# The last layer of a four-layer model: expert tiles written back to their tokens at once and spread over more slots, value products moved between two pairs of scores

## The reference, cut to what matters

```python
# attention, 16 heads of 8 features, causal
qkv = (xn @ W_qkv + b_qkv).reshape(b, s, 16, 24)        # q, k, v of each head
attn = softmax(where(k_pos > q_pos, -inf, q @ k.T / sqrt(8)))
a = (attn @ v).reshape(b, s, 128) @ W_out + b_out
# experts: 8 of them, each token uses the two with the largest probability
probs = softmax(xn @ router_w.T);  top_p, top_i = top_k(probs, 2)
cw = one_hot(top_i) * top_p / (top_p.sum() + 1e-8)
for e in range(8):
    out += cw[:, e] * (gelu(xn @ w1[e].T + b1[e]) @ w2[e].T + b2[e])   # 128 -> 512 -> 128
x = x + a + out
```

## Time and profile before

| | |
|---|---|
| runs | 2456.61, 2458.77, 2468.96 us; median 2458.77 |
| profiled execution | span 2438.6 us from its first to its last instruction; what lies around it is not in the trace |
| mean granted TensorE clock | 0.899 of full speed |
| PE busy | 1961.1 us (80%) |
| DVE busy | 1854.7 us (76%) |
| ACT busy | 1448.4 us (59%) |
| POOL busy | 1318.1 us (54%) |
| layer 3's slots 3 to 15 | 1738.3 to 2358.8 us |
| its slots 16 to 18 | 2358.8 to 2438.6 us |

### The profile page before, as it was taken

The page is one execution under the profiler, slowest core; times in us unless marked ns, Lnnn a source line. Parts: engine busy times, 40 slices in busy tenths (PEclk is TensorE's granted clock), DMA queues, the critical chain, the costliest instruction groups (busy, mean ns, idle before and its releaser), DMA issues. The chain is left out here.

```text
span 2438.6 us, 32864 instructions
## 1 busy us (share of the span) xinstructions
PE 1961.1 (80%) x10212; PEld 1020.8 (42%) x10212; DVE 1854.7 (76%) x2464; ACT 1448.4 (59%) x2630; POOL 1318.1 (54%) x962
## 2 busy tenths in 40 slices
PE   6797797979797977879857999656688889898876
PEld 5233343433343333335625777532244544454322
DVE  6499999999999999878787888757465555645752
ACT  2676777767777775563546666312566566655655
POOL 5599999989898989322324554327411111111653
PEclk9898999989898988989888999855899998999978
DMA  2354444545444545300200000022222322322211
GB/s 72 99 160 138 155 144 146 150 154 164 140 142 146 157 140 158 123 27 1 85 0 1 0 0 0 5 76 83 82 75 83 108 77 66 92 68 76 57 44 30
DMA packets 150288, 214.84 MB, mean 88 GB/s; under 512 B 30970, under 2 KB 62612, under 8 KB 149524
## 3 DMA queue, kind: packets, MB, share of 16 engines
q1 hardware_dynamic: 146052, 204.72, 27.8%
q0 software_dynamic: 4096, 8.40, 1.3%
HBM read 193.91 MB, written 23.86 MB: 89 GB/s over the span
## 5 line engine op out<-in xcount | busy, mean ns | idle before, releaser
L717 PE MATMUL ps<-m_hC,ident 128*128 128x512 f32 x1024 | 518.0, 651 | 127.7 <-DVE m_hC L1005 127.7
L914 POOL TENSOR_TENSOR m_dBx<-m_du,m_rowB 128x1024 f32<-128x1024 f32 x256 | 604.0, 2391 | 5.9 <-DMA m_rowB<-bc_rows 5.6
L2909 DVE TENSOR_REDUCE a_mx<-ps 128x2 f32<-128x1024 f32 (+2 forms) x320 | 351.6, 1117 | 183.6 <-PE ps L2571 142.5
L2770 ACT ACTIVATE a_pT<-ps 128x512 f32<-128x512 f32 (+2 forms) x640 | 319.8, 553 | 287.2 <-PE ps L2593 279.5
L840 ACT ACTIVATE ps<-m_delta,m_A 128x512 f32<-128x512 f32 x512 | 339.7, 685 | 119.5 <-DVE m_h L996 118.6
L717 PEld LDWEIGHTS ps<-m_hC,ident 128*128 128x128 f32 x1024 | 207.1, 209 | 423.9 <-issue 237.3
L3056 POOL TENSOR_SCALAR_AFFINE_SELECT a_pT<-a_pT 128x512 f32<-128x512 f32 x128 | 81.5, 636 | 472.0 <-ACT a_pT L2770 471.5
L996 DVE TENSOR_TENSOR_SCAN m_h<-ps,m_carry,m_dBx 128x512 f32<-128x512 f32 x256 | 311.2, 1265 | 9.0 <-ACT ps L840 9.0
L996 DVE TENSOR_TENSOR_SCAN m_h<-ps,m_dBx 128x512 f32<-128x512 f32 x256 | 295.9, 1206 | 18.8 <-ACT ps L840 18.2
L924 POOL TENSOR_TENSOR m_hC<-m_h,m_rowC 128x1024 f32<-128x1024 f32 x80 | 194.6, 2433 | 70.4 <-DVE m_h L996 70.0
L1005 DVE TENSOR_TENSOR m_hC<-m_h,ps 128x1024 f32<-128x1024 f32 x176 | 214.9, 1221 | 21.2 <-ACT ps L850 7.2
(11 more groups left out here) (404 smaller groups left out, 3568.8 us busy)
## 6 DMA issues: line engine op xcount, KB each, us to landing
m_rowB<-bc_rows SPq DMA_DIRECT2D x256, 256.0 KB, 4.4
m_rowC<-bc_rows SPq DMA_DIRECT2D x256, 256.0 KB, 4.0
a_w<-in_L3f_w1T SPq DMA_DIRECT2D x39, 256.0 KB, 2.7
a_w<-in_L3f_w2T SPq DMA_DIRECT2D x39, 256.0 KB, 3.4
qk_parts<-a_part SPq DMA_DIRECT2D x24, 256.0 KB
expert_rows<-in_zero_rows SPq DMA_DIRECT2D x39, 128.0 KB, 2.6
a_xs<-expert_rows SPq DMA_DIRECT2D x39, 128.0 KB, 2.3
expert_out<-a_y SPq DMA_DIRECT2D x39, 128.0 KB, 3.3
```

The source lines that it names most:

```text
L717: mm = pe.matmul(ps[:, bankY + c, :], k.ident[:], hC[:, n % NBUF, c, :], start=False, stop=n % NS == NS - 1)
L914: pool.tensor_tensor(dBx[:, n % NBUF], du[:, i % 2, :, chunk(i, x)], rowB[:, n % 4, :].unsqueeze(1).to_broadcast([P, HALF, CH]), ALU.mult) ...
L2770: act.activation(dst, src, ACT.Exp).then_inc(t_read, 1)
L2909: dve.tensor_reduce(mx[:, c % 2, :, es[0]:es[0] + len(es), t, x // CH], src, AX_X, ALU.max)\
```

## The change

1. `scatter` now carries 129 words for each row: the token's 128 features and, in word 128, its place in the result (the token's number for its first expert, the number plus 4096 for its second). `expert_rows` is 129 words wide, its padding rows are filled from a larger input with numbers past 8191, and POOL adds 4096 to the numbers between the 32nd and the 33rd scatter, after waiting for the first 32 to land.
2. DVE casts a tile's 2 x 128 numbers to integers (`back`) when XT has arrived. Instead of SP's `store_tile` POOL issues two indirect DMAs for each tile (`put`), which write its rows to their tokens' places. `ys` has six buffers instead of two and lies in the space of `xn`. The puts of a slot's tiles come in groups 4 to 6 of the next slot; those of the last slot's tiles in groups 8 to 10 of slot 16.
3. The 64 gathers go. SP loads each sequence's rows with two plain DMAs of 512 KB (`bring`) after all puts have landed, two sequences ahead of `combine` at most. All four combines are in slot 17 (groups 6, 8, 10, 11).
4. The tiles go over slots 3 to 16: three in each, two in slots 5, 9 and 15.
5. In each group `sums` of the group before it comes between pair A and pair B, not after B; XT and DOWN come after B, DOWN last in the group. Group 4 takes four score pieces (groups 5 and 6 one each), and three of them lie between the UPs of its tiles.

```diff
-SHARE = (2, 2, 1, 1, 2, 2, 2, 2, 2, 2, 1, 1)
+SHARE = (2, 2, 1, 1, 4, 1, 1, 2, 2, 2, 1, 1)
-FIRST_SLOT, LAST_SLOT = 3, 12
+FIRST_SLOT, LAST_SLOT = 3, 16
-GATHER = {LAST_SLOT + 1 + n: n for n in range(B)}
+TILES_IN = (3, 3, 2, 3, 3, 3, 2, 3, 3, 3, 3, 3, 2, 3)
+COMBINE = {6: 0, 8: 1, 10: 2, 11: 3}
@@ SP
-                def store_tile(kt):
...
+                def bring(n):
+                    if n >= 2:
+                        sp.wait_ge(combined, (n - 1) * 16)
+                    for r in range(2):
+                        first = r * TOK + n * S
+                        sp.dma_start(got[:, n % 2, r], R["out_rows"][first:first + S, :].rearrange("(j p) d -> p j d", p=P))\
+                          .then_inc(s_g[n % 2], 16)
...
+                for u in range(NY):
+                    sp.wait_ge(s_y[u], 32 * len(range(u, NTILE, NY)))
+                for n in range(B):
+                    bring(n)
@@ PE, in a group (scoreT(b, g, 0) and the first score stand before this)
+                        if back and g > 0:
+                            sums(b, g - 1)
+                        if g == 0 and 0 <= b - 1:
+                            sums(b - 1, GROUPS - 1)
+                        if back and len(TU[g]) > 2:
+                            scoreT(b, g, 2)
                         for j, kt in enumerate(tiles_of(s)):
                             if g == j:
                                 turn_rows(kt)
-                            if g == 7 + j:
-                                down(kt)
-                        if back and len(TU[g]) > 2:
-                            scoreT(b, g, 2)
-                        for i in units[1:]:
+                        for i in units[1:] if g != BURST else ():
                             score(f, i)
...
-                        if back and g > 0:
-                            sums(b, g - 1)
...
+                        for j, kt in enumerate(tiles_of(s)):
+                            if g == 7 + j:
+                                down(kt)
                         if g == BURST:
+                            between = iter(units[1:])
                             for kt in tiles_of(s):
                                 for x in range(2):
                                     up(kt, x)
+                                    if x == 1:
+                                        for i in itertools.islice(between, 1):
+                                            score(f, i)
@@ DVE
+                    dve.tensor_copy(R["back"][:, 2 * kt:2 * kt + 2], xs[:, kt % 4, :, D])
...
+                        if s == SLOTS - 1 and g in COMBINE:
+                            combine(COMBINE[g])
-                    if s - 1 in GATHER:
-                        combine(GATHER[s - 1])
@@ POOL
+                def put(kt):
+                    pool.wait_ge(s_read, s_at["DOWN", kt] + 1)
+                    for a in range(2):
+                        pool.indirect_dma_start(R["out_rows"], bass.IndirectOffsetOnAxis(
+                            ap=R["back"][:, 2 * kt + a:2 * kt + a + 1], axis=0), ys[:, kt % NY, a, :], None)\
+                            .then_inc(s_y[kt % NY], 16)
...
+                        if n == NT:
+                            pool.wait_ge(R["scattered"], 16 * NT)
+                            pool.tensor_scalar(R["xn"][:, :, D], R["xn"][:, :, D], float(TOK), None, ALU.add)\
+                                .then_inc(numbered, 1)
+                            pool.wait_ge(numbered, 2)
...
+                            for j, kt in enumerate(tiles_of(s - 1)):
+                                if g == 4 + j and s < LAST_SLOT + 1:
+                                    put(kt)
+                            for j, kt in enumerate(tiles_of(s)):
+                                if g == 8 + j and s == LAST_SLOT:
+                                    put(kt)
```

105 lines of the change are left out of this document (51 added, 54 removed).

## The result

The changed kernel takes 2452.39 us (median of 20 runs, 2443.11 to 2460.59), the kernel before in the same session 2459.78. The ratio is 0.9974, with a 95% interval of 0.9962 to 0.9987. By the ratio that is 6.4 us less (the two medians lie 7.4 apart), a third of the 19 that were forecast. The profiled execution took 2455.94 us with a span of 2454.2.

A forecast was written before the change was run, and what follows sets the result against it. Slots 0 to 2 were taken as bound by POOL, groups with `down` by PE. Terms -14.3 - 10.8 - 13 + 2.4 + 6 + 7 + 3 = -19.7, taken as -19, gave 2440 us (-0.8%), range 2420 to 2462.

The forecast's parts named there:

- the sentence on the puts: Groups 4 to 6 of slots with tiles: POOL's 78 puts, 7.5 us a slot, fall where no mask is due: 0.
- The order: Slots 3 to 15: groups 5 and 6 fall from 7.22 to 4.8 us; taken as -1.0 a slot, -13 us.
- rival C: Slots with tiles: the order gives its whole -2.4 us a slot, time 2422 us; chance 0.15.
- Tiles and the excess of slots 14 and 15: Slots 3 to 15: three tiles leave for slot 16, -14.3 us; slots 14 and 15 lose their excess, -10.8 us.
- Slot 2: Slots 0 to 2: POOL is the bound, and the wait ahead of the 33rd scatter adds 2.4 us (0 to 4).
- The end: Slot 16 onward: +6 us for slot 16, +7 for late combines, +3 for slow passes.
- Slot 16: Slot 16 with three tiles and late puts between masks takes 40.8 us instead of 34.9: +6 (3 to 9).
- the +7: Slot 17: four combines in a chain, waiting for loads, end 7.2 us late and delay the last `norm`: +7 us.
- the +3: Behind the last `norm`: ten more projection pass pairs at half clock, 0.31 us each: +3 us (0 to 5).
- Rival A: Slots with tiles: the order gives nothing, as mask waits and a slower burst eat the gain; 2453 us; chance 0.20.
- D: Scatters in slots 0 to 2: the wider row costs POOL time, up to 0.95 us a scatter, 2501 us; chance 0.08.
- B: The end: a longer chain, loads of 9 us a pair (+7), slot with puts +3, slow passes +2; 2452 us; chance 0.12.

The follow-up runs named there:

- paced kernel: Changed kernel with GpSimd waiting, ahead of each tile's two puts, until ScalarE has done that group's exponentials: 2426.68 us, ratio 0.9833; on the quick chip 0.9944.
- c_seg: Changed kernel with the first 32 scatters counted in two semaphores, so the wait ahead of the 33rd is split: 2452.15 us, ratio 0.9978.
- d_tail: Changed kernel with the four combines moved to slot 17 behind groups 4, 5 and 6 and to slot 18: 2446.60 us, ratio 0.9942.
- h_best: Changed kernel with split scatter wait, combines moved to groups without masks, and the old place of `sums` in slots without tiles: 2434.32 us, ratio 0.9882.
- three tiles a slot with the three repairs: Changed kernel with split scatter wait, old `sums` place without tiles, three tiles in slots 3 to 15, combines in slots 16 and 17: 2428.46 us, 0.9854.

## Why the prediction was wrong, step by step

**The step that failed is the sentence on the puts**: "POOL's puts, 78 at the scatter's 0.95 + 0.30, lie in groups 4 to 6, where no mask is due and group 4 alone lasts 10 us; 7.5 a slot: 0." I asked whether GpSimd had time and who waits for it. It has, and nobody does. But six of them in a row hold up two other engines, which cost 27 us instead of 0. No row of the first profile showed this. Its execution lay 20.2 us under the median, which I took for time around the span, where the profile of after has 1.7 us around its own. That was a sign that most executions contain something that this one lacked, among it VectorE's stops in slots 0 and 2.

**The order**: -13 was too small. In slots 3 to 12 the kernel before with the order takes 489.4 us, without it 512.4: -2.3 a slot, which is what rival C said, and for thirteen slots about -30. In the paced kernel groups 5 and 6 take from 2175.78 to 2180.76 (the second half of the row at 2179.68 is group 7's), 4.98 us for the forecast 4.8 and the 7.22 before. In the changed kernel itself they take 7.35 in slot 12, since its clock falls behind the hold-up. Slots with merged work gained most, 52.2 to 52.6 us instead of 56.0 to 57.8 in three of four; the sum had them like the others. The rule that without tiles the order costs nothing ("2.6, what the old order gives in slot 13") was wrong: the order everywhere has 0.9961, the order beside tiles alone 0.9873.

**Tiles and the excess of slots 14 and 15** (-14.3 and -10.8) fit: paced, plain slots with three tiles take 41.0 us for 41.5, slot 14 48.1, slot 15 37.1. Together with -30 that makes -55; from 623.7 to 562.1 are -61.6, on two chips.

**Slot 2**: +2.4 became 5.5 in the traces (49.8 to 55.3). The landing was taken as 2.6 us, but the 2.6 are those of SyncE's DMAs of 128 KB that zero the tensor; a scatter's landing was in no row. The wait for the first 32 holds GpSimd for 5.5 us here and for up to 7.7 in the other kernels that keep it. How much of it reaches the end is open, since without it (`c_seg`) the time stayed.

**The end**: +16 became +22.6 (80.1 to 102.7). Slot 16 came as priced, 39.8 us for 40.8. Slot 17 took 43.9 where the kernel before has 26.9 to 29.1. The expectations above have 40.9 for it, counted from its second pair of exponentials. The chain of four combines was not late (from the first one's end to the third's start 5.9 us, 5.7 priced), and it is not what the last `norm` waited for, so the +7 had the wrong path. The prediction's second estimate for a pair of loads, 4.4 us, fell shorter of the 5.9. The figures that it takes from the Trainium skill (DMA: Bandwidth & Descriptors, "Anatomy of one DMA") are given there for DMAs that GpSimd issues, and SyncE issues these loads. It was the masks beside the combines that held the slot up: with the combines moved or with one input slot 17 takes 35.1. What is left over 29 goes with a low clock, 0.76 in `d_tail` and 0.61 in `h_best` (35.3), and the order's part in that is not separated. "Nothing in the trace loads 512 KB" was a misreading: the first profile has such loads in earlier layers, with 5.1 and 7.3 us to landing. Behind the last `norm` 16.9 us pass, against 14.4 in the first profile of the kernel before and 16.6 in the second, so the traces do not say whether the +3 was there.

The parts as the traces have them: -61.6 + 27.0 + 5.5 + 22.6 = -6.5, against -6.4 by the ratio (closer than single profiles from several chips warrant). A hold-up of 27 at 0 and slots 3 to 15 that gave 23.5 more than their -38.1, 17 of it the order, nearly cancel; what is left of the miss is the end and slot 2. That the forecast missed by only 13 us is therefore luck. Rival A is refuted by the order's own runs, D by the scatter's 0.96 us. B's time (2452) came true, but not by its slow loads. Beyond both kernels lie, by ratio, the paced version (0.9833) and three tiles a slot with the three repairs (0.9854); both together ran only on the quick chip (0.9854).

## What to carry to other kernels

Price an indirect DMA not only on the queue that issues it: look at what ScalarE and VectorE do behind the last of a run of six or more without pauses, and break the run with a wait that costs nothing. Keep two-input SBUF work of VectorE away from GpSimd's stretches, or at least keep its pieces short. When the profiled execution is well under the timed runs, look for what most executions have and this one hasn't before subtracting anything from it. And before a length is laid to an edit, compare the granted clock of the two stretches: here the same instructions took 28.5 us at a clock of 0.88 and 34.9 at 0.61.
